# Second mixture through DRAM: 16 blocks of two experts, row transfers of 48 and 112, scatters padded to 128 partitions

## The reference: what must be computed

```
probs = softmax(x_flat @ Wg);  vals, idx = top_k(probs, 2);  vals = vals / sum(vals)
a = idx.reshape(BTK);  pos = number of earlier picks of the same expert
keep = pos < C                      # C = ceil(1.25 * 1088 / 32) = 43
buf[a * C + pos] = x_flat[token]    # dropped where keep is false
h = relu(buf @ W1 + b1);  o = h @ W2 + b2
y = sum of the two gathered rows, each times vals * keep
y = x_flat where both picks were dropped
```

## Time and profile before

| | us |
|---|---|
| median of 3 runs | 239.47 (238.03 to 240.11) |
| the profiled execution's own time | 237.12 |
| its span | 235.3 |
| first mixture, first scatter to last result row joined | 53.4 to 116.4 |
| attention, first score matmul to last residual | 128.8 to 170.9 |
| routing of the second mixture, to the slots | 170.9 to 181.0 |
| second mixture, first gather to last combine | 182.0 to 230.0 |
| last turn, sum and stores | 230.0 to 235.3 |

### The profile page before, as it was taken

One profiled execution on the slowest core, in us unless ns is written; L12 is line 12 of the kernel. 1 busy time (PEld: TensorE's weight loads), 2 busy tenths in 40 slices (PEclk: granted clock), 3 DMA queues, 4 the chain that ended last, 5 costly groups with the idle time before them and its releaser, 6 DMA issues.

```text
span 235.3 us, 4407 instructions
## 1 busy us (share of the span) xinstructions
PE 211.2 (90%) x1612; PEld 164.9 (70%) x1615; DVE 119.1 (51%) x415; ACT 79.8 (34%) x231; POOL 52.6 (22%) x86
## 2 busy tenths in 40 slices
PE   6999999898996999997898797998886999999982
PEld 3956568786765999996655777996643776776661
DVE  0071479774501332312850466666259658664942
ACT  2003525444269555530047112333321231321301
POOL 8043041007780544460300000001160000000000
PEclk9979999965589999999999799999999599999998
DMA  6959994981113699103069100000000000000001
GB/s 213 262 140 291 307 356 118 375 338 32 47 44 71 170 368 353 59 33 91 17 203 437 74 3 0 4 0 3 0 0 0 3 0 0 4 0 0 0 3 47
DMA packets 14711, 26.29 MB, mean 112 GB/s; under 512 B 4486, under 2 KB 9014, under 8 KB 14434
## 3 DMA queue, kind: packets, MB, share of 16 engines
q1 hardware_dynamic: 13010, 24.07, 30.2%
q0 software_dynamic: 1680, 1.94, 3.7%
HBM read 21.38 MB, written 4.81 MB: 111 GB/s over the span
## 4 chain that ended last, share of the span: by engine, by line
PE 76%; DVE 10%; ACT 6%; DMA 4%; issue 2%; POOL 0%; DVEq 0%; SPq 0%
PE ps L1303 72%; PE ps L1313 2%; DMA patchesT<-in_patchesT 1%; DMA o_tok<-o_rows 1%; PE ps L1677 1%; ACT attnT L728 1%; DVE dots_m L1110 1%; DMA o_rows<-o_sb,result_row 1%; ACT hid_b L703 1%; DVE h L1068 1%; DVE bn L787 1%; PE ps L1550 1%; ACT L697 1%; ACT L696 1%; ACT aoT L734 0%
## 5 line engine op out<-in xcount | busy, mean ns | idle before, releaser
L505 POOL TENSOR_TENSOR ln_rstd<-ln_var,minus_half 119x1 f32<-119x1 f32 x15 | 8.3, 557 | 69.8 <-DVE ln_var L795 69.6
L703 ACT ACTIVATE hid_b<-ps,w_ring 128x128 f32<-128x128 f32 x64 | 18.1, 365 | 10.9 <-PE ps L1303 7.1
L1241 DVE TENSOR_SCALAR back<-ps,slot_col 128x272 fp32r<-128x272 f32 x32 | 15.7, 497 | 11.6 <-PE ps L1303 11.6
L537 POOL DMA_INDIRECT o_rows<-o_sb,result_row x16 | 15.5, 970 | 20.7 <-DVE o_sb L1043 20.7
L580 ACT COPY xT<-ps 128x119 f32<-128x119 f32 (+1 forms) x20 | 4.9, 251 | 41.9 <-PE ps L1313 35.5
L1303 PE MATMUL ps<-w_ring,hid_b 128*128 128x128 f32 x128 | 17.1, 277 | 1.2 <-ACT hid_b L703 1.2
L1303 PE MATMUL ps<-xbT,w_ring 128*128 128x128 f32 x128 | 16.8, 275 | 0.0
L1303 PEld LDWEIGHTS ps<-w_ring,hid_b 128*128 128x128 f32 x128 | 15.5, 192 | 1.7 <-ACT hid_b L703 1.7
L1043 DVE TENSOR_TENSOR o_sb<-ps,b_all 128x128 f32<-128x128 f32 x16 | 4.7, 292 | 23.3 <-PE ps L1303 19.2
L1303 PE MATMUL ps<-filler 128*128 128x512 bf16 x45 | 14.2, 449 | 1.7 <-DVE filler L843 1.5
L1303 PEld LDWEIGHTS ps<-xbT,w_ring 128*128 128x128 f32 x128 | 15.5, 192 | 0.0
(11 more groups left out here) (242 smaller groups left out, 427.7 us busy)
## 6 DMA issues: line engine op xcount, KB each, us to landing
w_ring<-in_w_routed SPq DMA_DIRECT2D x16, 514.0 KB
m<-in_m SPq DMA_DIRECT2D x2, 2048.0 KB, 10.1
rooms<-zeros SPq DMA_DIRECT2D x8, 330.0 KB, 7.1
patchesT<-in_patchesT SPq DMA_DIRECT2D x6, 272.0 KB, 4.8
xb<-rooms SPq DMA_DIRECT2D x16, 66.0 KB
w_s<-in_w_s SPq DMA_DIRECT2D x2, 512.0 KB, 7.5
w_qkv<-in_w_qkv SPq DMA_DIRECT2D x1, 768.0 KB
b_all<-in_b_all SPq DMA_DIRECT2D x1, 512.0 KB
```

The lines of the kernel that those rows point to most:

```text
L505: nc.gpsimd.tensor_tensor(ln_rstd[:, g:g + 1], ln_var[:, g:g + 1], minus_half[:], ALU.pow).then_inc(rstd_ready, 1)
L537: nc.gpsimd.indirect_dma_start(o_rows[:], bass.IndirectOffsetOnAxis(ap=result_row[:, b:b + 1], axis=0), o_sb[:, b, :], None).then_inc(o_sc ...
L703: nc.scalar.activation(hid_b[:, b % RING, c, :], ps[:, b % 2, c * BS:(c + 1) * BS], ACT.Gelu, bias=w_ring[:, b % WRING, FF + c:FF + c + 1] ...
L1241: nc.vector.tensor_scalar(halves(back[:, (u // 2) % 8, :])[:, u % 2], ps[0:PAIR, 4 + u % 2, 0:HALF], slot_col[:, 0:1], None, ALU.is_equal) ...
```

## The change

**Routing inside the attention.** Softmax, top two and weights over all groups are replaced by steps for one group, set into the attention's lists: norm, turn (`router_turn`), copy, logits, the best two from the raw logits (`pick2`), marks in bf16 (`mark2`), ranks by small matmuls (`slot_ranks`), and the slot numbers (`place2`). The inverse root of groups 2 to 4 moves from POOL to ACT and DVE. The 30 fills are replaced by one run of 32, after the last group's ranks. The weights are computed after the last slot, from the gap of the two logits.

**By DRAM.** `scatter2` writes each group's rows twice to a table `rooms2` (32 experts, 1024 rows apart, the first 48 of each set to zero by one DMA early on): 10 indirect DMAs. SP loads 48 rows of each expert in three pieces (pairs 0-1, 2-7, 8-15), each as two transfers of 48 partitions. 16 blocks of two experts are turned, multiplied up, rectified by ACT, multiplied down, and biased by DVE; POOL scatters each block's 112 rows to `o_rows`. The results come back in transfers of 112 (64 for the last group) partitions with 1024 bytes each and two transfers for the remaining rows, on SP and ACT, and DVE makes the weighted sums. The stores are shared by SP and ACT.

**First mixture.** Both of its ends change: the scatters have 128 partitions (the added ones go to spare rows, by index tables loaded with the inputs), and the result rows are loaded in the new shape, the remaining rows by ACT.

Core of the diff:

```diff
-                        rooms[:], bass.IndirectOffsetOnAxis(ap=room[0:n, g, k:k + 1], axis=0),
-                        xm[0:n, g, k, :], None).then_inc(scattered, 16)
+                        rooms[:], bass.IndirectOffsetOnAxis(ap=room[:, g, k:k + 1], axis=0),
+                        xm[:, g, k, :], None).then_inc(scattered, 16)
...
-            picked_rows = o_rows[SPARE:, :].rearrange("(k t) d -> t k d", k=2)
             for g in range(G):
-                sp.dma_start(o_tok[0:rows(g), g, :, :], picked_rows[g * GT:g * GT + rows(g)]).then_inc(o_loaded[g], 16)
+                load_main(sp, o_tok, o_loaded[g], g)
...
+            act.wait_ge(o_scattered, 16 * NB)
+            load_rest(act, o_tok, o_rest_loaded)
...
+            sp.dma_start(rooms2.rearrange("(e r) d -> e r d", e=EM)[:, 0:TAKEN, :] ... zeros[0:EM, ...] ...).then_inc(rooms2_zero, 16)
+            sp.wait_ge(scattered2, 16 * 2 * G)
+            for p, (first, past_) in enumerate(PIECES):
+                for half in range(2):
+                    sp.dma_start(xb2[ROOM * half:ROOM * half + TAKEN, first:past_, :],
+                                 expert_rows[half, 0:TAKEN, first:past_, :]).then_inc(x2_loaded[p], 16)
+            sp.wait_ge(o2_scattered, 16 * PAIRS)
+            load_main(sp, o2_tok, o2_loaded[0], 0)
+            load_main(sp, o2_tok, o2_loaded[2], 2)
+            load_main(sp, o2_tok, o2_loaded[4], 4)
...
+            def scatter2(g):
+                pool.wait_ge(slot_ready, g + 1)
+                pool.wait_ge(xn_ready, 3 * G + g + 1)
+                for k in range(2):
+                    if k == 1:
+                        pool.wait_ge(xm_ready, G + g + 1)
+                    nc.gpsimd.indirect_dma_start(
+                        rooms2[:], bass.IndirectOffsetOnAxis(ap=slot[:, g, k:k + 1], axis=0),
+                        xm[:, g, k, :], None).then_inc(scattered2, 16)
+            def spread_rows2(j):
+                past_ = ROOM + TAKEN
+                pool.wait_ge(o2_ready, j + 1)
+                nc.gpsimd.indirect_dma_start(
+                    o_rows[:], bass.IndirectOffsetOnAxis(ap=result_row2[0:past_, j:j + 1], axis=0),
+                    o2_sb[0:past_, j, :], None).then_inc(o2_scattered, 16)
...
+            for j in range(PAIRS):
+                rectified(j)
+            act.wait_ge(o2_scattered, 16 * PAIRS)
+            load_rest(act, o2_tok, o2_rest_loaded)
+            load_main(act, o2_tok, o2_loaded[1], 1)
+            load_main(act, o2_tok, o2_loaded[3], 3)
...
-            fill(22, 2)
+            pe.wait_ge(h_joined, 4 * G)
+            fill(FILLS, 6)
...
+            for j in range(PAIRS):
+                if j + 2 < PAIRS:
+                    pair_turned(j + 2)
+                if j + 1 < PAIRS:
+                    pair_up(j + 1)
+                pair_down(j)
```

More of the change, by code:

```diff
@@ L174, in build @@
         pT = sb("pT", [HC * S, 2, 2, GT])
-        slots = sb("slots", [GT, G, EM])
         with ExitStack() as experts0:
@@ L761, in _ @@
                 for half in range(2):
-                    for e in range(half, CHUNK, 2):
-                        last = nc.scalar.activation(pre[:, e * SLOTS:(e + 1) * SLOTS],
-                                                    ps[:, 1, e * SLOTS:(e + 1) * SLOTS], ACT.Relu,
-                                                    bias=moe_b1[:, q * CHUNK + e:q * CHUNK + e + 1])
-                    last.then_inc(relu_ready, 1)
-                if q + 1 < QS:
-                    gathered(q + 1)
@@ L775, in _ @@
+            act.dma_start(out[LAST * GT + WHOLE_LAST:T, :], ymoe[WHOLE_LAST:rows(LAST), LAST, :]).then_inc(stored, 16)
         @blk.vector
@@ L1190, in _ @@
-            step(last)
-            for rws, gs, width in spans:
-                at = gs.start * EM
-                last = nc.vector.scalar_tensor_tensor(
-                    slots[0:rws, gs].rearrange("p g e -> p (g e)"), ps[0:rws, 5, at:at + width], float(FAR),
-                    second[0:rws, gs].rearrange("p g e -> p (g e)"), ALU.subtract, ALU.mult)
-            last.then_inc(slots_ready, 1)
-            nc.vector.tensor_tensor(weight[:], second[:], probs[:], ALU.mult).then_inc(weight_ready, 1)
@@ L1862, in _ @@
[L1862 to L1866 removed]
+            mix(0)
+            values(3)
+            values(4)
+            mix(1)
+            turn_probs(0)
+            dots(2)
+            mix2(0)
+            mix(2)
+            turn_probs(1)
+            turn_attn(0, 0)
+            turn_attn(0, 1)
@@ new lines, in _ @@
+            dots(3)
+            mix2(1)
+            attend(0)
+            mix(3)
+            turn_probs(2)
+            project(0)
+            turn_attn(1, 0)
+            turn_attn(1, 1)
+            dots(4)
+            mix2(2)
+            attend(1)
+            mix(4)
+            router_turn(0)
+            project(1)
+            turn_attn(2, 0)
+            router_logits(0)
+            turn_probs(3)
+            turn_attn(2, 1)
+            mix2(3)
+            slot_ranks(0)
+            attend(2)
```

952 lines of the change are left out of this document (455 added, 497 removed).

## The result

| | before | changed |
|---|---|---|
| median of 4 runs | 238.88 us (238.03 to 240.11) | 216.8 us (214.15 to 218.01) |
| the profiled execution | 237.12 us, span 235.3 | 214.15 us, span 212.3 |

The ratio is 0.9004, 95% interval 0.8898 to 0.9111. The median fell by 22.1 us where 21.0 were predicted; the spans of the two profiled executions differ by 23.0 us. The changed kernel was timed again three times later, beside runs of the kernel before on the same chip: 0.9235 (0.9042 to 0.9427), 0.9333 (0.9258 to 0.9407) and 0.9526 (0.9461 to 0.9592). (A ratio leaves out, on both sides, the executions that took over 1.5% longer than the fastest of the same kernel, so it is not the quotient of the two medians.)

The account below looks back on a forecast made before the run. PE set the time for 76% of the old span; POOL's scatters would bound the new pairs. Steps summed to a span of 214.3 against 235.3, -21.0, so 218.5 us from the median 239.47; range 214.8 to 223.5.

Parts of the forecast that it names:

- Ahead of the last residual: Everything up to the attention's last residual: it would end at 169.6 instead of 170.63, most added routing falling into gaps.
- rival C: Clock falls once in the attention's end or the pairs, making fills or pairs late: 222 us, chance 0.13.
- First mixture's scatters at 0: First mixture: ten scatters shorter by 0.1 us gain 0, being hidden by ACT's table loads.
- Its result load at -0.4: First mixture's load of result rows: -0.4 us, between -1.0 (transfer time halved) and +0.4 (ACT's second issue added).
- D: Attention does not hide the routing: last residual at 174 instead of 170, 222.5 us, chance 0.10.
- Routing of the last group 4.3: Behind the last residual: norm, turn, copy, logits, best two, marks, ranks and slots of the last group take 4.3 us.
- (2), (3): Second mixture: row scatters land 1.73 us later, at 178.4; SP's loads bring the first pairs' rows at 181.3.
- wait of the first pair for the fills: PE's 32 fills, 0.234 us each, 7.5 us in all, end about when the rows come, at 181.3.
- (5): Pairs: POOL's result scatters are the bound, 15 x 1.30 + 0.97 = 20.5 us, ending at 204.6.
- B: Scatters slower than the first mixture's, at 1.55 us each, beside a busier DVE or wider table: 223 us, chance 0.13.
- PE per pair 0.8: Pairs: PE needs 0.8 us a pair for turn, up and down, so it runs ahead of POOL's 1.30.
- The sign I had named for being wrong: POOL's row showing waits on DVE's `o_sb` in the pairs would mean PE, not POOL, is the bound.

Follow-up runs that it names:

- unpadded: Changed kernel with both mixtures' row scatters at 119 and 68 partitions and the pairs' scatters at 128 instead of 112: 217.38 us, unchanged kernel beside it 217.06.
- half_scatters: Changed kernel with only the odd pairs' results scattered, 8 scatters for 16: 217.86 us, against 223.76 for the unedited changed kernel.
- same_2: Changed kernel repeated without edit, on a chip without stalls: 217.06 us, ratio 0.9235 to the kernel before.
- same: Changed kernel repeated without edit, on the chip that showed stalls: 223.76 us, ratio 0.9526 to the kernel before.
- same_3: Changed kernel repeated without edit, on another chip without stalls: 217.98 us, ratio 0.9333 to the kernel before.
- fills22: Changed kernel with 22 fills instead of 32 behind the last ranks, on the chip with stalls: 225.1 us, ratio 0.9489 to the kernel before.
- fills0: Changed kernel with no fills instead of 32 behind the last ranks, on the chip with stalls: 226.81 us, ratio 0.9686 to the kernel before.
- fills22_2: Changed kernel with 22 fills instead of 32, again, on a chip without stalls: 216.43 us, ratio 0.9208 to the kernel before.

## Why the prediction was right, and where not

Residual at 165.95 and 46.35 us behind it make the span of 212.3; predicted were 169.6 and 44.7. The sum was right to 2 us because two errors went against each other (3.65 us too much up to the residual, 1.65 too little behind it), which is luck, and each step has to be looked at by itself.

**Ahead of the last residual: -4.7 us, predicted -1.0.** 1.66 us lie before the first row scatter and 0.70 us between it and the last result scatter, in code where the table's repeats differ as much from execution to execution. Of the attention's 2.66 us, 1.54 are a clock dip in the first trace of before (51.72 to 50.18) and 1.12 are the list (0.6 predicted). What the traces show as the change's own is this 1.1 and the 17.6 us behind the residual (63.9 to 46.35), together 18.7; the best runs of both on one chip are 18.0 apart. That the medians of the first series are 22.1 apart, so near the 21.0 of the forecast, is in part luck too. Of the changed kernel the fastest execution had been profiled (214.15, median 216.8), of the kernel before one with a low clock (0.931, where 0.970 occurs). I had taken all of the trace's 235.3 us as the kernel's own; 3.9 of them were dips. (A small misreading beside it: the dip that rival C puts at 49.6 us began by 49.25, and the third at about 182.2.)

**First mixture's scatters at 0: right** (unpadded: 23.55 against 23.60 us). **Its result load at -0.4: not seen.** The step "the transfers themselves have half the pieces" failed, in that it was counted as time saved ahead of the first sum. The three traces of the kernel before have 2.80 to 2.92 us there, the nine with the change 2.71 to 3.12, so it is +0.1 in the mean, and +0.2 in the first trace. SP's one long issue of 1.5 to 1.9 us stood in no term of mine. The Trainium skill's rule on how many engines a partition count uses ("DMA: Bandwidth & Descriptors", section on why a DMA increments its semaphore by 16), which gave -1.0, goes with the busier engines (0.78 against 0.50), but the time to the first sum did not follow it here.

**D, attention does not hide the routing: no**, as above. **Routing of the last group 4.3: 5.4.** Missed was DVE's order. Group 4's norm was ready for its reciprocal when ACT's root ended at 167.10 (166.81 + 0.29), but DVE did group 3's best two and marks first and came to it at 167.72, 0.6 us late. The ranks too are longer, ten small matmuls over 0.78 us where I had 0.6. And the sum had a hole: it took the norm to the start of the last step (172.32) and the turn from its end (172.7), so that the step's own 0.34 us are in neither term.

**By DRAM, step by step** (predicted, measured in the first trace):

| step | predicted | measured |
|---|---|---|
| (1) last two row scatters | 2.8 | 2.58 |
| (2), (3) landing, load, rows there | 4.6 | 3.87 |
| wait of the first pair for the fills | 0 | 2.26 |
| (4) first pair to first result scatter | 2.8 | 3.09 |
| (5) sixteen scatters | 20.5 | 19.50 |
| (6), (7) landing and result load | 4.0 | 3.94 |
| (8) ten sums | 3.3 | 3.45 |
| (9) stores | 2.4 | 2.25 |

The mechanism of (5) is the forecast's (half_scatters), with the pitch at 1.238 where I took 1.30: 112 partitions cost 0.93 us, less than any scatter of the trace of before. The one step that failed is the fills. I had them end with the rows at 181.3, at full clock; the rows came at 177.8 and the fills, half of whose time ran at clock 0.50, ended at 180.1. The term took the fills at the rate of the earlier trace rows, 0.234 us each, which is that of the full clock. This is rival C in small, at its place, and it repeats in same_2 (2.49), same (1.14) and same_3 (1.03). It took back more than the 1.95 us that (1) to (3) and (5) had given.

**B** (pitch 1.55) did not come: 0.92 to 0.95 us for all sixteen with DVE busy beside them; where the gaps grew, behind stalls or a low clock, POOL waited for DVE's `o_sb`, and its own issues stayed at 0.93. So what the Trainium skill says of DVE locking out GpSimd's descriptor writing ("DMA: Bandwidth & Descriptors", "SWDGE vs HWDGE vs iDMA") shows nowhere in these runs; whether any operation of DVE beside the scatters was of the kind that the page means, they do not show. **PE per pair 0.8** was too low: PE's list for a pair takes 1.07 us, with PE busy all the time (1.00 from 184 to 185 us), and POOL's margin over it is 0.17 us a pair, not 0.5. I had taken the rates of long rows of matmuls; here four of up take 0.61 us and not 0.48, four of down 0.44 and not 0.24. The sign I had named for being wrong, POOL waiting on `o_sb`, does appear in same, fills22, fills0 and fills22_2, each time behind a stall or a low clock.

**What stays open:** the source of the stalls of 1 to 2 us that one chip showed in four kernels. They end without a releaser in the program, in rows of ACT, PE and DVE; no run of the kernel before was traced there. All four kernels are the changed program or variants of it, and its times there rose by 7 us where those of the kernel before hardly rose, so the stalls may need both the chip and the changed program. Open as well is what makes SP's second issue of the result load so long, ACT's issues or the new shape.

## What to carry to other kernels

A profiled execution contains that execution's clock dips; before summing steps against it, look at the mean clock of every run shown and take the dips as a term of their own, or the gain is credited to the edit. Filler work ahead of a wait is a term with two rates: count it at the low clock too, and see what its late end was hiding (here the second piece of the rows) before shortening it. And when a resource bounds a stage, work out how far behind it the next one stands; here leaving out half of POOL's scatters freed 2.9 us of 20.

## What the hardware showed that I had not expected

- An indirect DMA's issue on POOL cost 1.07 us with 119 partitions and with 68 alike, 0.97 with 128 and 0.93 with 112, plus 0.30 us to the next.
- Five issues on SP took 1.76 us alone (119 partitions of 1024 bytes each), 2.17 with two rows of 512 bytes each, and 3.4 to 3.8 with 112 partitions and ACT's queue issuing beside it, of which one issue alone took 1.5 to 1.9. At the kernel's end, with the same shape and ACT issuing too, three took 1.36 and none was long.
- The same program took 216.8, 217.1 and 218.0 us (medians) in three series of runs and 223.8 in a fourth, on another chip; the kernel before, within one series, from 232.2 to 240.7.
- A run of 32 fills took 8.2 to 9.9 us in the seven traces that have it, and never ran at full clock from end to end; PE had waited several times just before.
